# Where three small products stand in a hand-scheduled transformer layer: folded values, state products and the order of GpSimd's normalizations

## Chip, core and metric

The kernel runs on one core of a Trainium2 chip. A core has five engines that run their own instruction streams side by side: TensorE (PE in the rows; PEld is its weight load), VectorE (DVE), ScalarE (ACT), GpSimd (POOL) and SyncE (SP), which issues the DMAs. They meet only through semaphores. The metric is the device time of one execution in microseconds (us); the median of several executions counts.

## What is computed

The reference is one decoder layer over 16 batches of 512 tokens of width 256, all in float32. Three sublayers follow one another, each with a residual and a layer norm:

```python
# 1: linear attention, 16 heads of 16; K = 2 key/value sets
states = einsum('kbhnd,kbhne->kbhde', ks, vs); state = prod(states, axis=0)
out = layernorm(einsum('bhnd,bhde->bhne', q, state)) * g + b;  x = layernorm(x + out @ Wo + bo)
# 2: cross attention, 16 heads of 64, 64 context rows per batch
attn = softmax(q @ k.T * 64**-0.5);  x = layernorm(x + (attn @ v) @ Wout.T + b_out)
# 3: eight experts (256 -> 1024 -> 256) that each take the first 1024 tokens with weight > 0
x = layernorm(x + combined)
```

## The kernel before

**Stages.** A setup stage prepares weights and the context's keys and values (until about 110 us of the profile), an attention loop computes sublayers 1 and 2 (to about 880 us), and the experts follow. The change is in the attention loop.

**The loop.** It runs over batches `it`, and in each over four slots of 128 tokens, tile n = 4·it + slot. One slot of the middle of the loop does for its tile: the scores `sim` (L137 to L139, three passes of split-float products, two halves h), their maximum and difference on DVE (`dve_max` L867, `dve_shift` L872), exp on ACT (L726), sums and reciprocal `rz` on DVE (L812, L816), the multiplication by `rz` on POOL (L968, two halves, "normalizes"), and, one tile late, the transposition of the probabilities `prob` into `pt` on PE (L497, two halves, `pe_pT`), the split of `pt` into `pT_hi` (ACT) and `pT_lo` (DVE L879) and the product with the folded values into `ob` (`pe_pB`). Around it run the linear attention of a later tile (`zb`, L524 to L526), three layer norms whose statistics are DVE's (L772, L774) and whose reciprocal root is POOL's (`pool_rstd`, `pool_rstd_twice`), and transpositions of `x` (`tr`).

**Preparations.** What a whole batch shares is made piece by piece between this work: `G`, `GT`, `R`, `T1`, `T0`, `ST`, `SB`, `SW`, `Q0`, `Q1` for the linear attention two batches ahead; `A0` to `A3` the folded keys of the next batch; `B0` to `B3` the folded values (`pw<-wox,vraw`, L454), used from slot 1 of their own batch. `ST` is the state products (`pw<-wk,t_sb`, L417, 32x32 tiles of the array, small products). From them DVE makes `s` (L762), POOL `sprod` and `sbdT` (L935, L938, `pool_state`), PE `SB` and `SW` (L427, L422), ACT and DVE their split `zw_hi`, `zw_lo` (L628, L745), and `zw` is used from the next batch on. A table written out by hand, `ORDER`, gives each preparation a (slot, place) on PE, on ACT and on DVE; the slot functions `pe_slot`, `act_slot`, `dve_slot` call `prep(place)` at fixed points. A pair such as `B0`, `B1` is one group of products on PE. All preparations share two accumulation banks, `pw0` and `pw1`, by turns; each waits until DVE or ACT has emptied the one before it on its bank. So `T1` waits for `B2`'s split, and `Q0` for `SB`'s.

**Queues.** Every engine works its stream in the written order. On POOL the end of slot 2 is `pool_state`, then `xb` (L912), then slot 3 begins with `pool_rstd_twice` (L899 to L907). ACT's output norms of slot 3 (L633 to `x2` and `o_sb`) wait for its `nmr`, and the split `zw_hi` is written behind them.

Of the kernel before, what the change touches and what calls it, by code (L numbers as in the profile page):

```python
# [27 lines left out]
P = 128  # L28
# [113 lines left out]
def setup_and_attention(nc, t, k, first, kv_scr, x2_scr, mask_scr, out_rows,  # L142
                        NB, S, C, NKV, MC, TPB, PAIRS, KEYS, HEADS, CAP, ffn_sizes):
    HK = KEYS // 2
# [49 lines left out]
    s = {n: k.sem(n) for n in (  # L194
        "x_loaded", "k_loaded", "v_loaded",
        "prep_made", "prep_hi", "prep_split", "prep_copied", "state_ready", "st_prod", "r_prod", "r_summed", "wv_split", "g_split",
        "tr_made", "tr_hi", "tr_taken", "xb_ready",
        "z_made", "z_taken", "x1_ready", "x1_biased",
        "sim_made", "max_made", "sim_taken", "exp_made", "sum_made", "rz_made", "p_ready",
        "pt_made", "pt_hi_made", "pt_taken", "o_made", "o_taken",  # L200
        "x2_ready", "out_ready", "x1_ones", "mask_in_a", *(f"x2_stored{i}" for i in range(4)), *(f"out_stored{i}" for i in range(4)),
        "bst0", "bst1", "bst2", "mv0", "mv1", "mv2",
# [4 lines left out]

    ORDER = {
# [9 lines left out]
    FIRST_ORDER = {  # L218
# [85 lines left out]
    def need(eng, name, value):  # L304

        if not isinstance(value, int) or value > 0:
            eng.wait_ge(s[name], value)
# [49 lines left out]
    def tile_exists(n):  # L357
        return not isinstance(n, int) or 0 <= n < NTILES
# [170 lines left out]
    def parts(it, slot):  # L529

        n = 4 * it + slot
        isint = isinstance(it, int)
        has_sim = not isint or 0 <= it < NB
        has_z = not isint or 0 <= it + 1 < NB
        has_prev = not isint or 1 <= n <= NTILES
        has_xT = not isint or TPB <= n + 8 < NTILES
        has_x1T = not isint or 0 <= n + 3 < NTILES
        return has_sim, has_z, has_prev, has_xT, has_x1T
# [100 lines left out]
    def has_state(it):  # L639

        return within(it + 2) and not (isinstance(it, int) and it == -2)
# [219 lines left out]
    def by_head(ap):  # L861
        return ap.rearrange("p (g j) -> p g j", j=NKV)
# [20 lines left out]
    def pool_rstd(pool, ln, n, q):  # L883

        counted[f"mv{ln}"].wait_next(n + 1)
        pool.tensor_scalar(ve[:, q, ln:ln + 1], mv[:, ln, q, 1:2], EPS, None, ALU.add).then_inc(s[f"ve{ln}"], 1)  # L886
        pool.wait_ge(s[f"ve{ln}"], n + 1)

        need(pool, ("z_taken", "x1_ready")[ln], n - 1)
        pool.tensor_tensor(rstd[:, q, ln:ln + 1], ve[:, q, ln:ln + 1], epsc[:, 0:1], ALU.pow).then_inc(s[f"rstd{ln}"], 1)  # L890
        if ln:
            counted[f"rstd{ln}"].wait_next(n + 1)
            pool.tensor_scalar(nmr[:, q, ln:ln + 1], mv[:, ln, q, 0:1], rstd[:, q, ln:ln + 1], -1.0,
                               ALU.mult, ALU.mult).then_inc(s[f"nmr{ln}"], 1)

    def pool_rstd_twice(pool, n, q):

        counted["mv2"].wait_next(n + 1)
        pool.tensor_scalar(ve[:, q, 2:3], mv[:, 2, q, 1:2], EPS, None, ALU.add)  # L899
        pool.tensor_scalar(ve[:, q, 3:4], mv[:, 2, q, 1:2], 1.0 + EPS, EPS * EPS, ALU.mult, ALU.add).then_inc(s["ve2"], 1)  # L900
        pool.wait_ge(s["ve2"], n + 1)

        need(pool, "x2_ready", n - 1)
        need(pool, "out_ready", n - 1)
        pool.tensor_tensor(rstd[:, q, 2:4], ve[:, q, 2:4], epsc[:, :], ALU.pow).then_inc(s["rstd2"], 1)
        counted["rstd2"].wait_next(n + 1)
        pool.tensor_scalar(nmr[:, q, 2:4], rstd[:, q, 2:4], mv[:, 2, q, 0:1], -1.0, ALU.mult, ALU.mult).then_inc(s["nmr2"], 1)  # L907

    def pool_xb(pool, n, b, slot, q):
        need(pool, "x_loaded", 16 * (b + 1))  # L910
        need(pool, "z_taken", n - 1)
        pool.tensor_tensor(xb[:, slot % 2, :], xraw[:, q, slot, 0:C], bprime[:, :], ALU.add).then_inc(s["xb_ready"], 1)  # L912

    def pool_x1_bias(pool, n, slot, par):

        need(pool, "tr_made", n + 5)
        x1_tile = x1[:, par(1 if slot else 0), (slot - 1) % 4, 1:C + 1]
        pool.tensor_tensor(x1_tile, x1_tile, boutbc[:, :], ALU.add).then_inc(s["x1_biased"], 1)  # L918

    def pool_split(pool, it):  # L920

        need(pool, "prep_copied", number(it, "GT", COPIED))
        pool.tensor_tensor(g_lo[:, :], g_sb[:, :], f32(g_hi[:, :]), ALU.subtract)
        pool.tensor_tensor(g10_lo[:, :], g10[:, :], f32(g10_hi[:, :]), ALU.subtract).then_inc(s["g_split"], 1)

    def pool_sums(pool, it):

        need(pool, "prep_copied", number(it, "R", COPIED))
        pool.tensor_tensor(r_prod[:, :, :], wvT[:, :, :], s_bc[:, :].unsqueeze(1).broadcast_to([P, 2 * MC, C]),
                           ALU.mult).then_inc(s["r_prod"], 1)  # L930

    def pool_state(pool, it):

        need(pool, "prep_split", number(it, "ST", FINISHED))
        pool.tensor_tensor(sprod[:, :, :], s01[:, 0, :, :], s01[:, 1, :, :], ALU.mult).then_inc(s["st_prod"], 1)  # L935
        pool.wait_ge(s["st_prod"], it + 3)
        need(pool, "prep_made", number(it - 1, last_of("SW", "SB")))
        pool.tensor_tensor(sbdT[:, :, :].rearrange("p m (g e) -> p m g e", g=4),  # L938
                           sprod[:, :, :].unsqueeze(2).broadcast_to([P, MC, 4, QW]),
                           blockmask[:, :].rearrange("p (g e) -> p g e", g=4).unsqueeze(1).broadcast_to([P, MC, 4, QW]),  # L940
                           ALU.mult).then_inc(s["state_ready"], 1)

    def pool_slot(pool, it, slot, e):
        par = lambda a: (e + a) % 2
        has_sim, has_z, has_prev, has_xT, has_x1T = parts(it, slot)
        n = 4 * it + slot
        q = slot % 2
        if tile_exists(n - 2):
            pool_rstd_twice(pool, n - 2, q)
        if (it, slot) == (-1, 3):  # L950
            pool_state(pool, it)
        if it == -1:
            pool_rstd(pool, 0, n + 4, q)
        if it == -1:
            pool_rstd(pool, 1, n + 4, q)
            pool_xb(pool, n + 5, it + 1 if slot < 3 else it + 2, (slot + 1) % 4, par(1 if slot < 3 else 2))
        if (it, slot) == (-1, 3):
            for j in range(1, 4):
                pool_x1_bias(pool, n - 3 + j, j, par)
        if has_x1T and it != -1:  # L960
            pool_x1_bias(pool, n, slot, par)
        if has_z and it != -1:
            pool_rstd(pool, 0, n + 4, q)
        if has_sim:
            need(pool, "rz_made", n + 1)
            for h in range(2):
                part = by_head(prob[:, q, h * HK:(h + 1) * HK])
                pool.tensor_tensor(part, part, rz[:, q, h * 8:h * 8 + 8].unsqueeze(2).broadcast_to([P, 8, NKV]),  # L968
                                   ALU.mult).then_inc(s["p_ready"], 1)
        if has_z and it != -1:  # L970
            pool_rstd(pool, 1, n + 4, q)
        if slot == STATE_SLOT and has_state(it) and it != -1:
            pool_state(pool, it)
        if tile_exists(n + 5) and it != -1:
            pool_xb(pool, n + 5, it + 1 if slot < 3 else it + 2, (slot + 1) % 4, par(1 if slot < 3 else 2))
        if slot == SPLIT_SLOT and has_state(it):
            pool_split(pool, it)
        if slot == SUMS_SLOT and has_state(it):
            pool_sums(pool, it)
        if (it, slot) == (NB - 1, 0):  # L980
            need(pool, "prep_made", number(NB - 3, last_of("SW", "SB")))
            ff["pool_small"](pool)
        if (it, slot) == (NB - 1, 0):
            ff["pool_weights"](pool, 0, 0, 0)
# [56 lines left out]
    prob = k.sb("prob", [P, 2, KEYS])  # L1041
    mx = k.sb("mx", [P, HEADS])
    zsum = k.sb("zsum", [P, HEADS])
    rz = k.sb("rz", [P, 2, HEADS])
# [859 lines left out]
```

## Time and profile before

| | |
|---|---|
| median of 3 runs | 1239.56 us (1238.46 to 1239.6) |
| the profiled execution | 1244.09 us, span of its instructions 1242.4 us |
| busy share: PE, PEld, DVE, ACT, POOL | 97%, 85%, 69%, 45%, 47% |
| granted TensorE clock, mean | 0.99 |
| one batch in the middle, slots 0 to 3 | 12.48, 11.95, 10.93, 13.12 us |

The slot lengths are the distances between the starts of the first transposition (`pt<-ident,prob`) of each slot, here from 500.00 to 548.48 us. A busy PE is not a PE at its peak, because the ends of matmuls are modelled; the starts of consecutive instructions tell more, and a start that comes later than the usual spacing is a stall. The batches from 172 to 778 us repeat each other within 0.2 us, so one of them can be read for all.

### The profile page before, as it was taken

Reading aid. Unit: us, or ns where it says so; the run is one execution under the profiler, and the core shown is the slowest. Engines: PE = TensorE matmul, PEld = TensorE weight load, DVE = VectorE, ACT = ScalarE, POOL = GpSimd, SP = SyncE. Lnnn points to the kernel's source line nnn. Section 1 sums busy time; section 2 is a strip of 40 time slices with the busy share of each in tenths; the row PEclk is TensorE's granted clock in tenths of the full one; section 3 lists DMA queues with packets and bytes.
Section 4 is the critical chain, followed back from the end, with each engine's and each line's share of the span. In section 5 each row is a group of like instructions: output and inputs, shape, how many; then the busy total and the mean of one; then the engine's idle time right before and its main releaser. Section 6 shows DMA issues by size and latency. Waiting matters only on the chain.

```text
span 1242.4 us, 27256 instructions
## 1 busy us (share of the span) xinstructions
PE 1203.1 (97%) x10512; PEld 1051.2 (85%) x10512; DVE 863.1 (69%) x1694; ACT 555.1 (45%) x1097; POOL 585.8 (47%) x968
## 2 busy tenths in 40 slices
PE   8987999999999999999999999989999999999998
PEld 7866888888888888888888888877799899899888
DVE  5545988889889889889898898988523423432435
ACT  2124556555555555465555555545523412421420
POOL 2223665666666666656666565655322112202201
PEclk9988999999999999999999999999999999999999
DMA  9821011021111011110211111310211022021001
GB/s 274 222 65 35 12 59 54 26 60 45 35 52 53 26 61 36 43 61 19 61 44 36 52 53 35 115 50 26 95 69 69 1 69 69 1 69 69 1 1 35
DMA packets 88739, 70.07 MB, mean 56 GB/s; under 512 B 41378, under 2 KB 82083, under 8 KB 88612
## 3 DMA queue, kind: packets, MB, share of 16 engines
q1 hardware_dynamic: 86580, 67.67, 18.0%
q8 instruction: 85, 1.39, 0.5%
q10 hardware_dynamic: 2032, 0.66, 0.2%
q14 instruction: 42, 0.34, 0.1%
HBM read 42.09 MB, written 26.22 MB: 55 GB/s over the span
## 4 chain that ended last, share of the span: by engine, by line
PE 71%; DVE 8%; issue 7%; POOL 6%; ACT 1%; POOLq 0%; DVEq 0%
PE sim L137 6%; PE sim L138 6%; PE sim L139 6%; PE ob L137 5%; PE ob L138 5%; PE ob L139 5%; PE pt L497 4%; PE pw L391 3%; PE pt L139 2%; PE pt L138 2%; PE pt L137 2%; PE pw L137 2%; PE pw L454 2%; PE pw L138 2%; PE pw L139 2%
## 5 line engine op out<-in xcount | busy, mean ns | idle before, releaser
L1619 POOL TENSOR_TENSOR w_lo<-w_raw,w_hi 128x2048 fp32r<-128x2048 f32 x16 | 73.8, 4614 | 220.9 <-ACT w_hi L1559 167.8
L137 PE MATMUL ob<-b_hi,pT_hi 128*128 128x256 f32 x512 | 151.0, 295 | 0.5 <-DVE pT_lo L879 0.5
L138 PE MATMUL ob<-b_lo,pT_hi 128*128 128x256 f32 x512 | 143.6, 280 | 0.0
L139 PE MATMUL ob<-b_hi,pT_lo 128*128 128x256 f32 x512 | 143.6, 280 | 0.0
L968 POOL TENSOR_TENSOR prob<-prob,rz 128x512 f32<-128x512 f32 x128 | 131.1, 1046 | 12.6 <-DVE rz L816 12.6
L732 ACT ACTIVATE pT_hi<-pt 128x512 fp32r<-128x512 f32 x128 | 76.2, 595 | 111.2 <-PE pt L497 110.6
L726 ACT ACTIVATE prob<-prob 128x512 f32<-128x512 f32 x128 | 81.1, 633 | 99.1 <-DVE prob L872 99.0
L137 PEld LDWEIGHTS ob<-b_hi,pT_hi 128*128 128x128 f32 x512 | 96.9, 189 | 9.0 <-issue 5.4
L138 PEld LDWEIGHTS ob<-b_lo,pT_hi 128*128 128x128 f32 x512 | 97.1, 190 | 1.9
L139 PEld LDWEIGHTS ob<-b_hi,pT_lo 128*128 128x128 f32 x512 | 96.3, 188 | 0.0
L867 DVE TENSOR_REDUCE mx<-sim 128x8 f32<-128x512 f32 x128 | 87.8, 686 | 6.6 <-PE sim L139 4.4
L886 POOL TENSOR_SCALAR ve<-mv 128x1 f32<-128x1 f32 x128 | 28.0, 219 | 136.3 <-DVE mv L774 136.2
L633 ACT ACTIVATE x<-h,nmr,rstd 128x256 f32<-128x256 f32 x128 | 76.5, 598 | 34.4 <-POOL nmr L907 17.2
L497 PE MATMUL pt<-ident,prob 128*128 128x128 f32 x512 | 78.7, 276 | 13.5 <-POOL prob L968 12.0
L872 DVE TENSOR_TENSOR prob<-sim,mx 128x512 f32<-128x512 f32 x128 | 88.3, 690 | 3.9
L1594 ACT ACTIVATE hT_hi<-zb 128x512 fp32r<-128x512 f32 x30 | 17.8, 592 | 159.8 <-PE zb L139 159.8
L879 DVE TENSOR_TENSOR pT_lo<-pt,pT_hi 128x512 fp32r<-128x512 f32 x128 | 86.7, 678 | 1.9 <-ACT pT_hi L732 1.7
L497 PEld LDWEIGHTS pt<-ident,prob 128*128 128x128 f32 x512 | 59.9, 140 | 27.4 <-POOL prob L968 16.3
L918 POOL TENSOR_TENSOR x<-x,boutbc 128x256 f32<-128x256 f32 x64 | 43.9, 688 | 79.6 <-PE tr L474 75.2
L812 DVE TENSOR_REDUCE zsum<-prob 128x16 f32<-128x1024 f32 x64 | 77.8, 1215 | 4.1 <-ACT prob L726 0.7
L890 POOL TENSOR_TENSOR rstd<-ve,epsc 128x1 f32<-128x1 f32 x128 | 72.1, 563 | 10.9 <-POOL ve L886 0.2
L1838 DVE SCALAR_TENSOR_TENSOR hT_lo<-sim,hT_hi 128x512 fp32r<-128x512 f32 x62 | 42.8, 691 | 44.3 <-ACT hT_hi L1594 44.3
(244 smaller groups left out, 3726.5 us busy)
## 6 DMA issues: line engine op xcount, KB each, us to landing
xraw<-in_x SPq DMA_DIRECT2D x16, 512.0 KB, 4.0
kv_scratch<-stage SPq DMA_DIRECT2D x32, 256.0 KB, 3.6
x_scratch<-x SPq DMA_DIRECT2D x64, 128.0 KB, 1.7
out_x<-o_sb SPq DMA_DIRECT2D x64, 128.0 KB, 1.7
w_raw<-in_L_ffn_experts_inter SPq DMA_DIRECT2D x8, 1024.0 KB, 5.1
w_raw<-in_L_ffn_experts_out SPq DMA_DIRECT2D x8, 1024.0 KB, 7.8
kraw<-kv_scratch SPq DMA_DIRECT2D x16, 256.0 KB, 2.9
vraw<-kv_scratch SPq DMA_DIRECT2D x16, 256.0 KB, 2.8
```

Source lines behind the costliest of these rows:

```text
L137: pe.matmul(out, lh, rh, start=first, stop=False)
L138: pe.matmul(out, lh, rl, start=False, stop=False)
L139: return pe.matmul(out, ll, rh, start=False, stop=last)
L497: last = pe.transpose(pt[:, r * P:(r + 1) * P], prob[:, par_n, c:c + P], ident[:, :])
L633: act.activation(dst, src, ACT.Identity, bias=nmr[:, q, ln:ln + 1], scale=rstd[:, q, ln:ln + 1]).then_inc(s[done], 1)
L726: act.activation(prob[:, q, h * HK:(h + 1) * HK], prob[:, q, h * HK:(h + 1) * HK], ACT.Exp).then_inc(s["exp_made"], 1)
L732: act.activation(pT_hi[:, h * 4:h * 4 + 4, :], pt[:, :].rearrange("p (r u) -> p r u", u=P), ACT.Copy).then_inc(s["pt_hi_made"], 1)
L812: dve.tensor_reduce(zsum[:, :], prob[:, q, :].rearrange("p (g j) -> p g j", j=NKV), AX.X, ALU.add).then_inc(s["sum_made"], 1)
L867: dve.tensor_reduce(mx[:, h * 8:h * 8 + 8], by_head(sim[h][:, :]), AX.X, ALU.max).then_inc(s["max_made"], 1)
L872: dve.tensor_tensor(by_head(prob[:, q, h * HK:(h + 1) * HK]), by_head(sim[h][:, :]), mx[:, h * 8:h * 8 + 8].unsqueeze(2).broadcast_to([P, ...
L879: dve.tensor_tensor(pT_lo[:, h * 4:h * 4 + 4, :], pt[:, :].rearrange("p (r u) -> p r u", u=P), f32(pT_hi[:, h * 4:h * 4 + 4, :]), ALU.subt ...
L968: pool.tensor_tensor(part, part, rz[:, q, h * 8:h * 8 + 8].unsqueeze(2).broadcast_to([P, 8, NKV]), ALU.mult).then_inc(s["p_ready"], 1)
```

## The change

Three edits. `B0`/`B1` move on PE from between the two halves of slot 0's `ob` product to behind them, right before slot 1's first transposition, and `B2`/`B3` from between the two halves of slot 1's scores to behind them, right before its second transposition; their places on ACT and DVE move with them. `ST` moves in slot 3 in the same way, on PE and on DVE. In slot 2 POOL multiplies the first half of the probabilities by `rz` ahead of the first layer norm's root, instead of behind it.

```diff
@@ -207,12 +207,12 @@
-        "B0": ((0, 7), (0, 8), (1, 0)), "B1": ((0, 7), (0, 8), (1, 0)),
-        "B2": ((1, 1), (1, 1), (1, 3)), "B3": ((1, 1), (1, 1), (1, 3)),
+        "B0": ((0, 8), (1, 0), (1, 1)), "B1": ((0, 8), (1, 0), (1, 1)),
+        "B2": ((1, 2), (1, 3), (1, 5)), "B3": ((1, 2), (1, 3), (1, 5)),
...
-        "ST": ((3, 1), (3, 1), (3, 3)),
+        "ST": ((3, 2), (3, 1), (3, 5)),
@@ -911,6 +911,12 @@
+    def pool_p(pool, q, h):
+
+        part = by_head(prob[:, q, h * HK:(h + 1) * HK])
+        pool.tensor_tensor(part, part, rz[:, q, h * 8:h * 8 + 8].unsqueeze(2).broadcast_to([P, 8, NKV]),
+                           ALU.mult).then_inc(s["p_ready"], 1)
@@ -959,14 +965,16 @@
+        if has_sim and slot == 2:
+            need(pool, "rz_made", n + 1)
+            pool_p(pool, q, 0)
         if has_z and it != -1:
             pool_rstd(pool, 0, n + 4, q)
         if has_sim:
             need(pool, "rz_made", n + 1)
-            for h in range(2):
-                part = by_head(prob[:, q, h * HK:(h + 1) * HK])
-                pool.tensor_tensor(part, part, rz[:, q, h * 8:h * 8 + 8].unsqueeze(2).broadcast_to([P, 8, NKV]),
-                                   ALU.mult).then_inc(s["p_ready"], 1)
+            if slot != 2:
+                pool_p(pool, q, 0)
+            pool_p(pool, q, 1)
         if has_z and it != -1:
             pool_rstd(pool, 1, n + 4, q)
```

On DVE, slot 3, the piece of the difference around `s`, which DVE makes from the state products; L867 is `dve_max`, L872 `dve_shift`:

```order
 L867 TENSOR_REDUCE mx<-sim 128x8
 L872 TENSOR_TENSOR prob<-sim,mx 128x512
+L867 TENSOR_REDUCE mx<-sim 128x8
+L872 TENSOR_TENSOR prob<-sim,mx 128x512
 L762 SCALAR_TENSOR_TENSOR s<-bkq,r_sb,pw 128x32 x4
-L867 TENSOR_REDUCE mx<-sim 128x8
-L872 TENSOR_TENSOR prob<-sim,mx 128x512
 L879 TENSOR_TENSOR pT_lo<-pt,pT_hi 128x512
 L849 TENSOR_TENSOR tT_lo<-tr,tT_hi 128x512
```

The second half's maximum and difference now stand ahead of `s`. On PE in the same slot, the rows around the state products before:

```order
L138 MATMUL sim<-a_lo,tT_hi 128x512
L139 MATMUL sim<-a_hi,tT_lo 128x512
L417 MATMUL pw<-wk,t_sb 32x32 x32
L137 MATMUL sim<-a_hi,tT_hi 128x512
L138 MATMUL sim<-a_lo,tT_hi 128x512
L139 MATMUL sim<-a_hi,tT_lo 128x512
```

and of the change:

```order
L138 MATMUL sim<-a_lo,tT_hi 128x512
L139 MATMUL sim<-a_hi,tT_lo 128x512
L417 MATMUL pw<-wk,t_sb 32x32 x32
L497 MATMUL pt<-ident,prob 128x128 x4
L470 MATMUL tr<-ident,x 128x128 x2
L474 MATMUL tr<-ident,xraw 128x128 x2
```

They have the transpositions behind them now, not six more score products. On POOL, from the end of the first norm's work in slot 2 to `pool_state`, before:

```order
L918 TENSOR_TENSOR x<-x,boutbc 128x256
L886 TENSOR_SCALAR ve<-mv 128x1
L890 TENSOR_TENSOR rstd<-ve,epsc 128x1
L968 TENSOR_TENSOR prob<-prob,rz 128x512 x2
L886 TENSOR_SCALAR ve<-mv 128x1
L890 TENSOR_TENSOR rstd<-ve,epsc 128x1
L893 TENSOR_SCALAR nmr<-mv,rstd 128x1
L935 TENSOR_TENSOR sprod<-s 128x64
L938 TENSOR_TENSOR sbdT<-sprod,blockmask 128x256
```

and of the change:

```order
L924 TENSOR_TENSOR x<-x,boutbc 128x256
L917 TENSOR_TENSOR prob<-prob,rz 128x512
L886 TENSOR_SCALAR ve<-mv 128x1
L890 TENSOR_TENSOR rstd<-ve,epsc 128x1
L917 TENSOR_TENSOR prob<-prob,rz 128x512
L886 TENSOR_SCALAR ve<-mv 128x1
L890 TENSOR_TENSOR rstd<-ve,epsc 128x1
L893 TENSOR_SCALAR nmr<-mv,rstd 128x1
L941 TENSOR_TENSOR sprod<-s 128x64
L944 TENSOR_TENSOR sbdT<-sprod,blockmask 128x256
```

One of the two multiplications has moved ahead of `ve` and `rstd`; `pool_state` stays where it was.

## Rows read from the trace of the kernel before

**Rows 1.** The page: busy time, share of the span, instructions of each engine
```profile
PE 1203.1 (97%) x10512; PEld 1051.2 (85%) x10512; DVE 863.1 (69%) x1694; ACT 555.1 (45%) x1097; POOL 585.8 (47%) x968
```

**Rows 2.** Waits from 172.6 to 778.1 us: total us, times, longest
```profile
PEld pw L137 <- DVE zw_lo L745: 3.1, 12, 0.3
PE pt L497 <- POOL prob L968: 3.5, 12, 0.3
```

**Rows 3.** Timeline of PE, slot 2 into 3: start, us, instruction, [idle before]
```profile
534.79 0.28 PE L139 MATMUL ob<-b_hi,pT_lo 128*128 128x256 f32 x1
535.36 0.65 PE L497 MATMUL pt<-ident,prob 128*128 128x128 f32 x4 [0.29 <-POOL prob L968]
```

**Rows 4.** Timeline of POOL and DVE, end of slot 2
```profile
532.59 0.25 DVE L816 RECIPROCAL rz<-zsum 128x16 f32<-128x16 f32 x1
533.44 0.22 POOL L886 TENSOR_SCALAR ve<-mv 128x1 f32<-128x1 f32 x1 [2.51 <-DVE mv L774]
534.26 2.05 POOL L968 TENSOR_TENSOR prob<-prob,rz 128x512 f32<-128x512 f32 x2
535.33 0.47 DVE L856 SCALAR_TENSOR_TENSOR h<-zb,rstd,xb 128x256 f32<-128x256 f32 x1
```

**Rows 5.** Timeline of DVE, slot 3
```profile
539.39 0.71 DVE L762 SCALAR_TENSOR_TENSOR s<-bkq,r_sb,pw 128x32 f32<-128x32 f32 x4
540.02 0.68 DVE L867 TENSOR_REDUCE mx<-sim 128x8 f32<-128x512 f32 x1
...
541.35 0.68 DVE L879 TENSOR_TENSOR pT_lo<-pt,pT_hi 128x512 fp32r<-128x512 f32 x1
...
545.14 1.12 DVE L745 TENSOR_TENSOR zw_lo<-pw,zw_hi 128x256 fp32r<-128x256 f32 x2
```

**Rows 6.** Timeline of POOL and ACT, slot 3
```profile
540.19 0.32 POOL L935 TENSOR_TENSOR sprod<-s 128x64 f32<-128x64 f32 x1 [2.38 <-DVE s L762]
540.59 0.74 POOL L938 TENSOR_TENSOR sbdT<-sprod,blockmask 128x256 f32<-128x256 f32 x1
...
543.38 0.27 POOL L907 TENSOR_SCALAR nmr<-rstd,mv 128x2 f32<-128x2 f32 x1
...
543.68 0.60 ACT L633 ACTIVATE x<-h,nmr,rstd 128x256 f32<-128x256 f32 x1 [1.10 <-POOL nmr L907]
```

**Rows 7.** Timeline of PE, second part of slot 3
```profile
542.73 0.29 PE L139 MATMUL ob<-b_hi,pT_lo 128*128 128x256 f32 x1
542.85 0.39 PE L427 MATMUL pw<-ident,sbdT 128*128 128x128 f32 x2
...
545.24 0.28 PE L139 MATMUL ob<-b_hi,pT_lo 128*128 128x256 f32 x1
545.58 0.50 PE L137 MATMUL pw<-tT_hi,wq_hi 128*128 128x512 f32 x1
```

**Rows 8.** Timeline of PE: what follows tiled products, and what follows plain ones
```profile
528.82 0.66 PE L497 MATMUL pt<-ident,prob 128*128 128x128 f32 x4
529.31 0.38 PE L470 MATMUL tr<-ident,x 128*128 128x128 f32 x2
...
538.02 0.50 PE L137 MATMUL sim<-a_even_hi,tT_hi 128*128 128x512 f32 x1
538.36 0.39 PE L138 MATMUL sim<-a_even_lo,tT_hi 128*128 128x512 f32 x1
...
539.28 0.39 PE L139 MATMUL sim<-a_even_hi,tT_lo 128*128 128x512 f32 x1
539.51 0.60 PE L497 MATMUL pt<-ident,prob 128*128 128x128 f32 x4
539.95 0.38 PE L470 MATMUL tr<-ident,x 128*128 128x128 f32 x2
```

**Rows 9.** Timeline of DVE and PE, slot 1
```profile
516.14 1.29 DVE L745 TENSOR_TENSOR b_lo<-pw,b_hi 128x512 fp32r<-128x512 f32 x2 [0.23 <-ACT b_hi L628]
517.35 0.68 DVE L867 TENSOR_REDUCE mx<-sim 128x8 f32<-128x512 f32 x1
518.81 0.39 PE L137 MATMUL pw<-wv_hi,g_hi 128*128 128x512 f32 x1
```

## The prediction

> **What bounds the kernel now.** I read the page first: TensorE is busy 97% of the span and no other engine over 69% [rows 1]. So the time is that of PE's stream plus its stalls, and a change of places can only take away stalls or switching costs, or add some. Next the waits of the regular part of the loop, twelve batches. Two releasers of PE come back in every batch, 12 times each: POOL's normalized probabilities ahead of a transposition, and DVE's `zw_lo` ahead of a product of `pw` [rows 2]. Then the timeline shows where they are.
>
> The first is at the start of slot 3. After an `ob` product the next instruction normally starts 0.12 us later (542.73 to 542.85 [rows 7]); here it starts 0.57 us later (534.79 to 535.36 [rows 3]), so the stall is 0.45 us. The second is `Q0`: it starts 0.34 us behind the last `ob` product (545.24 to 545.58 [rows 7]), 0.22 more than normal. It is small, but it says that `Q0` has no slack: whatever makes `zw_lo` late makes PE late by as much.
>
> What stands ahead of `zw_lo` is a chain through four engines in slot 3. DVE makes `s` at 539.39; POOL has waited 2.38 us for it and starts `sprod` at 540.19; being in order, POOL gets to the output norm only behind `sprod`, `sbdT` and `xb`, and its `nmr` starts at 543.38; ACT has waited 1.10 us for that and starts at 543.68 the two output norms that stand ahead of `zw_hi`; DVE starts `zw_lo` at 545.14 and PE `Q0` at 545.58 [rows 5 to 7]. From `s` to `Q0` are 6.19 us, with two engines idle on the way because they waited for the link before them.
>
> **The change part by part.**
>
> *POOL first in slot 2.* `rz` is finished at 532.59 + 0.25 = 532.84, while POOL idles until the norm's statistics arrive at 533.44 [rows 4]. The first half can start at about 532.93 (0.09 us for the semaphore, an estimate, from the 0.80 us between the start of `s`, four operations of 0.71 us together, and that of `sprod` [rows 5, 6]) and is done about 1.05 us later, half of the 2.05 of the pair: 533.98 instead of 534.26 + 1.05 = 535.31. PE wants it at 534.91. The wait goes, with 0.9 us to spare: 0.45 us less in this place. Its price: `rstd` comes later. It took 0.82 us from `ve` to the next instruction (533.44 to 534.26), so it is finished at about 533.98 + 0.82 = 534.8. DVE uses it at 535.33, behind other work [rows 4]. Nothing is late. The second half starts at 534.8 and ends at 535.8, before 534.26 + 2.05 = 536.3.
>
> *The neighbours on PE.* Products on parts of the array cost something on the way in and out. A score product behind the state products takes 0.34 us to the next start (538.02 to 538.36), against 0.23 for a plain one (539.28 to 539.51): 0.11 for the way out. Where tiled products stand ahead of transpositions already (`A0` in slot 2), the four transpositions take 0.49 us (528.82 to 529.31) against 0.44 behind plain scores (539.51 to 539.95) [rows 8]: 0.05 for the way out. The way in is the same at the old places and the new. So each of the three moves is worth 0.11 - 0.05 = 0.06 us where PE doesn't wait anyway; the bounds are 0 and 0.11, and I take 0.05, since this is the nearest row, rounded down. The Trainium skill (TensorEngine Tiling (Array Packing), Key Properties) says that changing the tiling mode drains the engine, whatever the neighbour; transpositions run on the full array as the scores do, so by that rule alone the moves would be worth 0, and the sum 1.2 us worse. The trace agrees that the switch costs, and shows it cheaper ahead of transpositions.
>
> *Folded values, slots 0 and 1.* Three engines are touched, so I followed them through slot 1. `B0`/`B1` are emptied by ACT and DVE at the head of slot 1 instead of across its border; in slot 1 DVE does the same operations in another order. DVE's split of `B2`, `B3` moves behind the second maximum and difference, some 1.33 us (540.02 to 541.35 for this pair [rows 5]). `B2`'s split started at 516.14, is two of 0.6 us each (1.21 to the next start at 517.35), and `T1` on its bank starts at 518.81 [rows 9]. Moved, the first of the two runs from about 517.5 to 518.2: 0.5 us before `T1`. All else of slot 1 that PE wants is further away. I cost these moves at nothing but their two gains, 0.05 each, 0.1 us per batch, and slot 3 starts 0.1 us sooner.
>
> *State products, slot 3.* This is the part that decides. On DVE `s` now stands behind the maximum and difference of the second half. These take 1.33 us from start to the next start (540.02 to 541.35) [rows 5], and DVE has no idle time there: it runs one operation after another from the folded keys of slot 2 on, so PE's being 0.45 us sooner doesn't make DVE sooner. `s` starts at 539.39 + 1.33 - 0.09 = 540.63 (the 0.09 are the moves of slots 0 and 1). All that is behind it moves with it, since POOL and ACT waited for it before: `sprod` 541.43, `sbdT` done at 540.59 + 0.74 + 1.24 = 542.57, `nmr` 544.62, ACT's output norms 544.92, `zw_lo` 546.38, `Q0` 545.58 + 1.24 = 546.82. PE meets it twice. It arrives at `SB` at 542.85 - 0.45 - 0.09 - 0.05 = 542.26, and waits 0.3 to 0.4 us for `sbdT`; at `Q0` it arrives at about 545.2 and waits 1.6 us. The 0.45 us that POOL gained in slot 2, and the state products' own 0.05, are lost in these waits.
>
> **The sum.** A batch gets 1.33 - 0.09 = 1.24 us longer. The state is made for a batch two ahead, so slot 3 has an `ST` in the batches 0 to 13 (for the one ahead of batch 0 the table has its own places, which don't change): 14 x 1.24 = 17.4 us. In the last two batches there is no `ST`; PE waits there for the probabilities, behind DVE's work, of which the sum per slot stays the same, and I put 0 with bounds of 1 us either way. The first of the 14 may lose 0.1 less. 17.3 us on the profiled execution's 1244.09 are 1261.4; that execution lies 4.5 us above the median of the runs, so on the median it is 1239.56 + 17.3 = 1256.9.
>
> **Rivals.**
>
> *The chain has slack (faster).* If `Q0` could take `zw_lo` 1.3 us later than now, only the gains would stay: 0.45 for the stall of slot 3 and 0.15 for the three moves: 0.60 x 14 = 8.4 us, 1231.2. For it speaks that the busy shares of POOL and ACT are under half [rows 1]. Against it, that `Q0` waits 12 times of 12 for `zw_lo` [rows 2]: it decides only if the delay of `s` at DVE were under 0.45 us or so. Chance 7%.
>
> *Only part of the delay arrives.* If another operation than `s` releases ACT or POOL in part (the `xb` or the norm statistics), the delay at `Q0` could be 0.5 to 1.1 us: 7 to 15 us, 1247 to 1254. The idle times of 2.38 and 1.10 us [rows 6] speak against it, since they are as long as the whole delay. 8%.
>
> *Slot 1 gets late too.* If ACT takes `B2` later than I think, `T1` waits. The 0.5 us margin is the smallest of the replay; where it is gone and as much again is lost, each batch pays 0.5 more: 7 us, 1264. 12%.
>
> *The folded values or POOL's order do nothing at all*, or cost their bound: 0 instead of 0.09 in a batch is 1.3 us, 1258. Inside the main case.
>
> **How the numbers follow.** The forecast as worked out, 1254 to 1260, has 70%; with slot 1 late 12% (1260 to 1266), part of the delay 8% (1247 to 1254), slack 7% (1229 to 1237), and 3% for a result within 0.2%. That bound, 2.5 us, is about what a measurement of this kernel can tell from no change. The range from 1249 to 1263 leaves out the faster case, the low part of the partial one and the top of the late one. Faster 7%, same 3%, slower 90%.
>
> **What the profile of the changed kernel would show.** The wait of the transposition for POOL's probabilities at the start of slot 3 is gone, and slot 2 is 10.5 us long instead of 10.93. POOL's idle time ahead of `sprod` is about 3.6 us instead of 2.38. PE waits for POOL's `sbdT` ahead of `SB`, 0.3 to 0.4 us, and for DVE's `zw_lo` ahead of `Q0`, some 1.6 us, in 14 batches; slot 3 is 14.9 us long instead of 13.12. Slots 0 and 1 are shorter by 0.04 to 0.05 us each. The prediction is wrong if `Q0` starts less than a microsecond later within its batch, which would mean that something other than `s` sets `zw_lo`; or if `T1` waits in slot 1.

## The result and the profile after

The change made the kernel slower: 1255.65 us in the median (1254.19 to 1256.13), beside 1239.58 us (1238.46 to 1240.93) for the kernel before on the same chip. The ratio is 1.0124, 95% interval 1.0111 to 1.0136. The forecast was 1257.0, in the range 1249 to 1263. Of the executions in this document one, of `s_early`, took 1960.28 us at a mean granted clock of 0.557; its ratio leaves it out.

The page's first part, and then the waits from 173.6 to 796 us (total us, times, longest us), a stretch with twelve `Q0` and thirteen `s`. They answer to [rows 1] and [rows 2].

```profile
PE 1196.0 (95%) x10512; PEld 1046.4 (83%) x10512; DVE 861.3 (69%) x1694; ACT 547.7 (44%) x1097; POOL 585.7 (47%) x968
```

```profile
POOL sprod L941 <- DVE s L762: 48.2, 13, 3.7
...
ACT x L633 <- POOL nmr L907: 36.6, 12, 3.1
...
DVE zw_lo L745 <- ACT zw_hi L628: 21.6, 12, 1.8
...
PEld pw L137 <- DVE zw_lo L745: 18.9, 12, 1.6
PE pw L137 <- DVE zw_lo L745: 16.5, 12, 1.4
```

No engine has more work than before. PE's busy share fell from 97% to 95%, because it stands still more. `Q0` (`pw L137`) waited 3.1 us in twelve batches before, 0.26 each (PEld's row, the weight load); now 18.9 us, 1.6 each, and PE itself 1.4. The list also shows the path of the delay: POOL waits 3.7 us for `s`, ACT 3.1 for POOL's `nmr`, DVE 1.8 for ACT's `zw_hi`, PE for DVE's `zw_lo`. The wait of a transposition for POOL's `prob` [rows 2, 3] is gone from the start of slot 3.

PE in slot 3, in order of time. It answers to [rows 7] and the last part of [rows 8]:

```profile
543.40 0.76 PE L417 MATMUL pw<-wk,t_sb 128*32 128x32 f32 x64
544.09 0.66 PE L497 MATMUL pt<-ident,prob 128*128 128x128 f32 x4
544.59 0.38 PE L470 MATMUL tr<-ident,x 128*128 128x128 f32 x2
...
548.00 0.41 PE L427 MATMUL pw<-ident,sbdT 128*128 128x128 f32 x2 [0.35 <-POOL sbdT L944]
...
552.07 0.50 PE L137 MATMUL pw<-tT_hi,wq_hi 128*128 128x512 f32 x1 [1.38 <-DVE zw_lo L745]
```

The slot began at 540.11. `SB` waits 0.35 us for `sbdT`, and `Q0` 1.38 us for `zw_lo`, both where the prediction put them. The four engines between `s` and `Q0`, DVE first, then POOL and ACT:

```profile
545.92 0.71 DVE L762 SCALAR_TENSOR_TENSOR s<-bkq,r_sb,pw 128x32 f32<-128x32 f32 x4
...
551.59 1.17 DVE L745 TENSOR_TENSOR zw_lo<-pw,zw_hi 128x256 fp32r<-128x256 f32 x2 [1.80 <-ACT zw_hi L628]
```

```profile
546.71 0.33 POOL L941 TENSOR_TENSOR sprod<-s 128x64 f32<-128x64 f32 x1 [3.71 <-DVE s L762]
...
549.90 0.27 POOL L907 TENSOR_SCALAR nmr<-rstd,mv 128x2 f32<-128x2 f32 x1
...
550.20 0.60 ACT L633 ACTIVATE x<-h,nmr,rstd 128x256 f32<-128x256 f32 x1 [3.05 <-POOL nmr L907]
...
551.20 0.84 ACT L628 ACTIVATE zw_hi<-pw 128x256 fp32r<-128x256 f32 x2
```

From the start of `s` to that of `Q0` are 552.07 - 545.92 = 6.15 us; before they were 6.19. The chain is as long as it was, within 0.04 us, and it starts later: `s` 1.22 us later within its batch in the mean of 13 batches, `Q0` 1.19 us.

**Where the time is in the whole.** A batch is measured from the first transposition of its slot 0 to that of the next batch. Over the 13 distances between batches 1 and 14 the mean is 48.548 us before and 49.735 after: 13 x 1.187 = 15.4 us. From the start of slot 1 of batch 0 to the start of batch 1 come 1.3 us more (37.25 instead of 35.97), the end of the program gives 0.8 back: 15.9, where the medians differ by 16.1. The 0.8 are in the two last batches, 0.1 in batch 14 and 0.7 in batch 15: there slot 1 takes 9.64 us instead of 10.61 and slot 2 11.04 instead of 10.72. `folded_only` and `st_back` show the same pair (9.65 and 11.05 us), so it comes from the folded values' places. Before, PE waited in that slot for the split of the probabilities; of the change no such wait is in the trace:

```profile
852.10 0.39 PE L137 MATMUL ob<-b_hi,pT_hi 128*128 128x256 f32 x1 [0.54 <-DVE pT_lo L879]
```

This sum leaves out the time up to the first slot 1, which differs between executions by several microseconds whatever the kernel (last section). For this reason the table goes by batches as well as by medians. The interval is that of the ratio to the kernel before, which ran again beside each group: median 1239.80 us beside `st_back`, `s_early`, `st_only` and `norm_first`, 1240.93 beside `s_half`, `pool_only`, `norm_first_before` and `norm_first_s_early`, 1238.96 beside the others.

| kernel | batch, us | slots 0 to 3, us | median, us | ratio, 95% |
|---|---|---|---|---|
| before | 48.548 | 12.49 11.98 10.96 13.12 | 1239.58 | |
| the change | 49.735 | 12.37 12.01 10.50 14.86 | 1255.65 | 1.0124 (1.0111 to 1.0136) |
| st_back | 48.455 | 12.38 12.01 10.50 13.57 | 1239.01 | 0.9986 (0.9970 to 1.0003) |
| s_early | 48.455 | 12.38 12.01 10.50 13.57 | 1237.46 | 0.9982 (0.9964 to 0.9999) |
| st_only | 49.881 | 12.52 11.98 10.96 14.43 | 1258.71 | 1.0148 (1.0119 to 1.0177) |
| s_half | 49.463 | 12.49 11.98 10.96 14.04 | 1253.85 | 1.0104 (1.0084 to 1.0123) |
| pool_only | 48.549 | 12.48 11.98 10.51 13.58 | 1239.64 | 0.9997 (0.9985 to 1.0009) |
| folded_only | 48.458 | 12.38 12.01 10.94 13.13 | 1236.76 | 0.9977 (0.9967 to 0.9986) |
| norm_first_before | 48.548 | 12.49 11.98 10.96 13.13 | 1239.81 | 1.0003 (0.9988 to 1.0017) |
| norm_first_s_early | 48.458 | 12.38 12.01 10.50 13.58 | 1235.43 | 0.9968 (0.9953 to 0.9983) |
| norm_first | 48.092 | 12.37 12.01 10.50 13.21 | 1233.79 | 0.9951 (0.9933 to 0.9969) |
| norm_first_again | 48.104 | 12.38 12.01 10.50 13.22 | 1232.63 | 0.9946 (0.9932 to 0.9961) |
| tr_first | 47.785 | 12.38 12.01 10.50 12.90 | 1227.83 | 0.9912 (0.9892 to 0.9932) |

### The profile page after: what moved, and what is told of

The parts are those of the page before. It is cut to its first block, busy times and chain, and to the rows that moved or that the text cites. A ratio compares the mean times of both kernels' runs of the same rounds, so it can differ in the third digit from the quotient of the medians.

```text
span 1254.0 us, 27256 instructions
## 1 busy us (share of the span) xinstructions
PE 1196.0 (95%) x10512; PEld 1046.4 (83%) x10512; DVE 861.3 (69%) x1694; ACT 547.7 (44%) x1097; POOL 585.7 (47%) x968
## 4 chain that ended last, share of the span: by engine, by line
PE 67%; POOL 10%; issue 9%; DVE 6%; ACT 3%; POOLq 0%; DVEq 0%
PE sim L137 6%; PE sim L138 6%; PE sim L139 6%; PE ob L137 5%; PE ob L138 5%; PE ob L139 5%; PE pw L391 3%; PE pt L497 3%; PE pw L137 3%; PE pt L139 2%; PE pt L138 2%; PE pt L137 2%; PE pw L454 2%; PE pw L139 2%; PE pw L138 2%
## 5 line engine op out<-in xcount | busy, mean ns | idle before, releaser
L137 PE MATMUL ob<-b_hi,pT_hi 128*128 128x256 f32 x512 | 149.5, 292 | 0.0
L137 PEld LDWEIGHTS ob<-b_hi,pT_hi 128*128 128x128 f32 x512 | 96.9, 189 | 2.9
L867 DVE TENSOR_REDUCE mx<-sim 128x8 f32<-128x512 f32 x128 | 87.5, 684 | 6.4 <-PE sim L139 4.4
L872 DVE TENSOR_TENSOR prob<-sim,mx 128x512 f32<-128x512 f32 x128 | 88.3, 690 | 3.9
L139 PE MATMUL pt<-w_hi,hT_lo 128*128 128x256 f32 x256 | 72.1, 281 | 0.0
```

The source lines that it names most:

```text
L137: pe.matmul(out, lh, rh, start=first, stop=False)
L139: return pe.matmul(out, ll, rh, start=False, stop=last)
L867: dve.tensor_reduce(mx[:, h * 8:h * 8 + 8], by_head(sim[h][:, :]), AX.X, ALU.max).then_inc(s["max_made"], 1)
L872: dve.tensor_tensor(by_head(prob[:, q, h * HK:(h + 1) * HK]), by_head(sim[h][:, :]), mx[:, h * 8:h * 8 + 8].unsqueeze(2).broadcast_to([P, ...
```

## The experiments

The theory is that of the prediction: `s` is late on DVE, POOL's queue passes this on to the output norm, and all of it arrives at `Q0`. The rivals are that the state products cost by their place on PE, that only a part of the delay arrives, and that slot 1 or POOL's new order is the cause.

### The state products back in both places, and on DVE alone

`st_back` is the change with `ST` as before; `s_early` leaves `ST` at its new place on PE and takes only DVE's `s` back.

```diff
-        "ST": ((3, 2), (3, 1), (3, 5)),
+        "ST": ((3, 1), (3, 1), (3, 3)),    st_back
+        "ST": ((3, 2), (3, 1), (3, 3)),    s_early
```

> The change, with the state products and s back in their old places on PE and DVE. If the chain from s to Q0 is the whole cause, slot 3's wait for sbdT and the long wait for zw_lo go; Q0 then starts where the unchanged chain lets it, about 0.09 us sooner per batch than before (the folded values' gain), and POOL's 0.45 us is still not seen, because Q0 already waited for zw_lo before. 14 x 0.07 to 0.09 = about 1 us: 1238 to 1239 (slots 0 to 3 about 12.37, 12.0, 10.48, 13.55). Rival, the folded values or POOL's order cost something: then 1242 or more. Rival, the chain had slack and POOL's gain is real once the state products are back: 0.45 + 0.1 in 14 batches, 1231 to 1233.

> The change, with only DVE's place of s put back ahead of the second maximum; PE keeps the state products behind the scores. It tells the order on DVE from the order on PE. If DVE's order is the cause: PE finishes the products about 0.4 us before DVE wants them, so s starts as in the kernel before, and the time is that of st_back within 1 us, 1238 to 1240. If the place on PE is the cause (products late or an expensive switch of the array), it stays at 1254 to 1256.

Both give a batch of 48.455 us, 1.280 less than the change and equal to each other within 0.001. So the place on PE is worth nothing to the batch, and the whole loss hangs on the two operations that were put ahead of `s`. `s_early`'s median, 1237.46 us, lies 0.5 below what I had expected (1238 to 1240). `st_back` from `s` to `Q0` (its slot 3 starts at 532.17):

```profile
536.65 0.71 DVE L762 SCALAR_TENSOR_TENSOR s<-bkq,r_sb,pw 128x32 f32<-128x32 f32 x4
...
539.61 0.38 PE L427 MATMUL pw<-ident,sbdT 128*128 128x128 f32 x2
...
542.84 0.50 PE L137 MATMUL pw<-tT_hi,wq_hi 128*128 128x512 f32 x1 [0.57 <-DVE zw_lo L745]
```

The same of `s_early` on PE (its slot 3 starts at 532.12):

```profile
539.50 0.38 PE L427 MATMUL pw<-ident,sbdT 128*128 128x128 f32 x2
...
542.80 0.50 PE L137 MATMUL pw<-tT_hi,wq_hi 128*128 128x512 f32 x1 [0.64 <-DVE zw_lo L745]
```

In `st_back` `s` and `Q0` start 6.19 us apart, as before. But `Q0` waits 0.57 us, more than before: slot 2 is 0.46 us shorter and slot 3 0.45 longer. What POOL saves in slot 2, PE stands still in slot 3. The same happens to the little that the new place of the state products does save: in `s_early` PE is at `SB` 7.38 us behind the slot's start instead of 7.44, and waits 0.64 us at `Q0` instead of 0.57.

### The state products alone

The kernel before with only `ST` at its new places.

```diff
-        "ST": ((3, 1), (3, 1), (3, 3)),
+        "ST": ((3, 2), (3, 1), (3, 5)),
```

> The kernel before, with only the state products and s at their new places. If the chain is the cause: s 1.33 us later in 14 batches, all of it at Q0, 14 x 1.33 = 18.6, minus nothing: 1257 to 1259, slower than the whole change by 1 to 3 us, and the stall of 0.45 us for the probabilities at the start of slot 3 is still there. If the three edits share the loss, it is clearly under 1255.

A batch is 1.333 us longer in the mean. One of the 13 distances has 0.43 us more in slot 0 than the others (50.33 us; cause unknown); without it the batch is 1.30 us longer. That is the start-to-start time of the moved pair (1.33 [rows 5]) less the 0.03 us by which the chain from `s` to `Q0` is shorter in the mean (6.17 us instead of 6.19). The median is 1.0148 times that before: this third of the change is worse alone than the whole. The slot's two old waits show what happens to the stall ahead of it:

```profile
539.65 0.65 PE L497 MATMUL pt<-ident,prob 128*128 128x128 f32 x4 [0.30 <-POOL prob L968]
...
551.15 0.50 PE L137 MATMUL pw<-tT_hi,wq_hi 128*128 128x512 f32 x1 [1.40 <-DVE zw_lo L745]
```

POOL's 0.30 is still there, and `Q0` waits as long as in the full change.

### Half of the delay

The kernel before, with `s` behind the second maximum but ahead of the second difference. A price with a threshold would show less than the delay here.

```diff
-        "ST": ((3, 1), (3, 1), (3, 3)),
+        "ST": ((3, 1), (3, 1), (3, 4)),
...
             dve_max(..., 1)
+        prep(4)
             dve_shift(..., 1)
```

> The kernel before, with s on DVE behind the second maximum but ahead of the second difference: half of the way, 0.72 us instead of 1.33. PE is untouched. If Q0's start follows s one to one, without slack: 14 x 0.72 = 10 us, 1249 to 1251, batch 49.27 us. If there is a threshold (some slack, then loss), it lies clearly below 10 us, or at nothing.

```profile
544.03 0.69 DVE L868 TENSOR_REDUCE mx<-sim 128x8 f32<-128x512 f32 x1 [0.26 <-PE sim L139]
544.63 0.71 DVE L762 SCALAR_TENSOR_TENSOR s<-bkq,r_sb,pw 128x32 f32<-128x32 f32 x4
...
550.79 0.50 PE L137 MATMUL pw<-tT_hi,wq_hi 128*128 128x512 f32 x1 [0.94 <-DVE zw_lo L745]
```

My expectation of `s` missed: it is 0.95 us later within its slot (4.98 instead of 4.03 us behind the slot's start), not 0.72, because the maximum, no longer behind `s`, is early and waits 0.26 us for PE's scores. The batch is 0.915 us longer, and the median, 1253.85, lies above my 1249 to 1251 for that reason. So the rule holds at a second size: 0.95 us of delay gave 0.915, and 1.33 gave 1.30. There is no threshold between.

### POOL's order alone, and the folded values alone

The kernel before with the edit of `pool_slot` alone, and with the places of `B0` to `B3` alone.

```diff
+        if has_sim and slot == 2:
+            need(pool, "rz_made", n + 1)
+            pool_p(pool, q, 0)                                             pool_only
...
-        "B0": ((0, 7), (0, 8), (1, 0)), ...  "B2": ((1, 1), (1, 1), (1, 3)), ...
+        "B0": ((0, 8), (1, 0), (1, 1)), ...  "B2": ((1, 2), (1, 3), (1, 5)), ...   folded_only
```

> The kernel before, with POOL's new order in slot 2 alone. The wait of 0.45 us at the start of slot 3 goes, slot 2 is 10.5 us. If Q0 is held by zw_lo and that by DVE's chain from slot 2, slot 3 gets as much longer: batch 48.55, 1239 to 1240, no change. If PE's own stream is the bound there, the gain is 0.45 x 14 = 6 us: 1233.

> The kernel before, with the folded values' new places alone. By the traces so far they are worth 0.09 us per batch, because the products stand next to transpositions: slot 0 at 12.37 to 12.38 instead of 12.49, slot 1 at 12.0 instead of 11.97, batch 48.46 instead of 48.55; 1.3 us in all, less than the runs can tell, 1237 to 1240. If what st_back gained came from POOL's order, the batch stays at 48.55.

`pool_only` shortens slot 2 by 0.45 us and lengthens slot 3 by 0.46; the batch is unchanged (48.549), the ratio 0.9997. The reason stands at `Q0`, whose weight load waited 0.26 us before and waits 0.78 now (6.2 us in eight batches, 300 to 700 us); PE itself waits 0.57:

```profile
541.09 0.50 PE L137 MATMUL pw<-tT_hi,wq_hi 128*128 128x512 f32 x1 [0.57 <-DVE zw_lo L745]
```

`folded_only` gains 0.090 us in a batch, all in slot 0 (-0.11), while slot 1 loses 0.03. The ratio is 0.9977, and its interval leaves out 1. The Trainium skill (TensorEngine Tiling (Array Packing), Key Properties) says that a change of tiling mode drains TensorE, and names no neighbour on which the price depends; by that alone this run would show 0. It shows a small gain instead, of the size of two moves at 0.05. The medians differ by 2.2 us, of which 14 batches explain 1.3; another 0.6 is in the last batch's slots 1 and 2, as told above.

### The output norm ahead of `s` in POOL's queue

If POOL's queue is what passes the delay on, it must vanish when the norm of slot 3 stands ahead of `sprod`. `norm_first` is the change with `pool_state` moved from the end of slot 2 to behind `pool_rstd_twice` in slot 3; `norm_first_before` makes the same edit in the kernel before.

```diff
-        if (it, slot) == (-1, 3):
+        if (it, slot) == (-1, 3) or slot == 3 and has_state(it):
             pool_state(pool, it)
...
-        if slot == STATE_SLOT and has_state(it) and it != -1:
-            pool_state(pool, it)
```

> The change, with POOL's pool_state moved behind the output norm of slot 3, so that the norm doesn't wait for s. If the chain from s to Q0 runs through POOL's order (s, sprod, sbdT, xb, norm, ACT's output norms, zw_hi, zw_lo), nmr2 comes before s, ACT is free when SB and SW are made, and Q0 starts when PE gets there: its wait of 1.4 to 1.6 us goes. PE still waits 0.35 us for sbdT. A batch is then 49.74 - 1.6 = 48.1 us, faster than before: 14 x (48.55 - 48.1) = 6 us less than before, 1232 to 1235. If zw_lo is late for another reason (the state products themselves, or DVE's own load), most of the wait stays and it is over 1245.

> The kernel before, with pool_state behind slot 3's output norm and nothing else. There zw_lo starts at 545.14 right behind DVE's own statistics, though zw_hi is there at the same time; DVE stood idle 0.59 us before it split tT, waiting for ACT. If that idle time is a second limit on zw_lo, as near as POOL's: no change, 1238.5 to 1240. If POOL's order is the only limit before the change too: 0.22 us per batch, 3 us, 1236.5.

`norm_first` is 1.643 us per batch faster than the change, and with 0.9951 faster than the kernel before. POOL, DVE and PE in its slot 3, which starts at 526.95:

```profile
531.90 0.27 POOL L907 TENSOR_SCALAR nmr<-rstd,mv 128x2 f32<-128x2 f32 x1
532.76 0.71 DVE L762 SCALAR_TENSOR_TENSOR s<-bkq,r_sb,pw 128x32 f32<-128x32 f32 x4
534.02 0.69 DVE L849 TENSOR_TENSOR tT_lo<-tr,tT_hi 128x512 fp32r<-128x512 f32 x1
534.84 0.41 PE L427 MATMUL pw<-ident,sbdT 128*128 128x128 f32 x2 [0.34 <-POOL sbdT L944]
...
537.37 0.40 PE L137 MATMUL pw<-tT_hi,wq_hi 128*128 128x512 f32 x1
```

`nmr` starts 0.86 us ahead of `s`, not 3.98 behind it. `Q0` no longer waits; what is left of the late `s` is PE's 0.34 us at `SB`.

`norm_first_before` changes nothing at all (48.548): of the two outcomes that I had named, no change and 3 us less, it is the first. There a second limit is as near as the one taken away:

```profile
535.29 0.69 DVE L849 TENSOR_TENSOR tT_lo<-tr,tT_hi 128x512 fp32r<-128x512 f32 x1 [0.59 <-ACT tT_hi L722]
```

DVE idles 0.59 us ahead of `tT_lo`, because ACT's `tT_hi` stands behind the exp of the second half, whose difference DVE makes only behind `s`. In the change DVE makes that difference first, and the gap is filled. Two further kernels take this up.

### Which of the two limits holds: `s` early again, and ACT's order

`norm_first_s_early` is `norm_first` with DVE's `s` back at (3, 3). `tr_first` is that kernel with ACT's transposition copy `tT_hi` ahead of its second exp, so that a late difference doesn't matter to `tT_lo`. `norm_first_again` repeats `norm_first` beside it.

```diff
+        if slot == 3:
+            act_tr(act, n, slot, has_x1T, has_xT)
             act_exp(act, n, q, 1)
...
-        if slot == 3:
-            act_tr(act, n, slot, has_x1T, has_xT)
```

> norm_first with s back at its early place on DVE. PE's wait for sbdT (0.35 us) goes. But the trace of st_back shows DVE idle 0.58 us ahead of the split of tT when s stands early, because ACT's exp and tT_hi wait for the second difference, which s delays; with s late that gap is filled. If this is the next limit, zw_lo starts 10.2 us after slot 3's start instead of 9.6, Q0 waits again, slot 3 is 13.5 instead of 13.2: 1237 to 1239, worse than norm_first by 4. If only the wait for sbdT counts, it is better than norm_first: 1228 to 1230.

> norm_first_s_early, with ACT's tT_hi of slot 3 ahead of its second exp. If DVE's idle 0.58 us ahead of the split of tT is what holds zw_lo there, it goes, zw_lo starts 9.65 us after slot 3's start instead of 10.22, and Q0 at 10.1, with no wait for sbdT ahead: slot 3 about 13.0, batch 47.87, 14 x 0.68 = 9.5 us less than before, 1229 to 1231, and better than norm_first by 3. If exp then comes late and sums with it, the gain is lost: 1235.

> norm_first once more, beside tr_first on the same chip: 1232 to 1235, batch 48.09.

`norm_first_s_early` falls back to 48.458: the gap on DVE is there again, and `Q0` waits 0.63 us. Its median, 1235.43, is lower than the 1237 to 1239 that I had expected; the batch is as expected (slot 3 13.58 us). DVE and PE:

```profile
536.06 0.69 DVE L849 TENSOR_TENSOR tT_lo<-tr,tT_hi 128x512 fp32r<-128x512 f32 x1 [0.59 <-ACT tT_hi L722]
...
538.58 0.99 DVE L745 TENSOR_TENSOR zw_lo<-pw,zw_hi 128x256 fp32r<-128x256 f32 x2
...
539.03 0.50 PE L137 MATMUL pw<-tT_hi,wq_hi 128*128 128x512 f32 x1 [0.63 <-DVE zw_lo L745]
```

`tr_first` takes the gap away with `s` early; its ACT, and then DVE and PE:

```profile
528.47 0.59 ACT L722 ACTIVATE tT_hi<-tr 128x512 fp32r<-128x512 f32 x1
529.41 0.63 ACT L726 ACTIVATE prob<-prob 128x512 f32<-128x512 f32 x1 [0.35 <-DVE prob L872]
```

```profile
529.29 0.68 DVE L879 TENSOR_TENSOR pT_lo<-pt,pT_hi 128x512 fp32r<-128x512 f32 x1
529.89 0.68 DVE L849 TENSOR_TENSOR tT_lo<-tr,tT_hi 128x512 fp32r<-128x512 f32 x1
...
532.85 0.50 PE L137 MATMUL pw<-tT_hi,wq_hi 128*128 128x512 f32 x1
```

`tT_lo` follows the row ahead of it without a gap. `Q0` starts 10.00 us behind the start of slot 3 (522.85), where `norm_first_s_early` has 539.03 - 528.36 = 10.67. The batch is 47.785 us: 0.673 less than `norm_first_s_early`, from which it differs in ACT's order alone, 0.32 less than `norm_first_again`, measured beside it, and 0.763 less than before. With 0.9912 and a median of 1227.83 (I had expected 1229 to 1231) it is the fastest kernel of the study. POOL's order in slot 2 and the folded values came with the change. ACT's order alone, without the norm moved ahead, was not run.

## Why the prediction was right, by its steps

The prediction named as its own refutation a `Q0` that starts less than a microsecond later within its batch, or a wait at `T1`. `Q0` starts 1.19 us later in the mean, and `T1` does not wait.

**`s` behind the pair, 1.33 us.** Shown. `s_early` takes back DVE's place alone and with it all of the loss; `st_only` costs 1.30 (1.333 with its one longer batch).

**The chain hands it on one to one through POOL's queue.** Shown: at two sizes by `st_only` and `s_half`, and for the place by `norm_first`, where the same late `s` no longer reaches `Q0`. The rival that only a part arrives falls.

**The folded values and neighbours, 0.05 for each move.** Right in the sum, wrong in the places. The prediction says 0.04 to 0.05 for each of slots 0 and 1; slot 0 gave 0.11 to 0.12 and slot 1 lost 0.03. In slot 0 the `ob` product behind `B0`, `B1` took 0.22 us to the next start, where plain ones take 0.12, and that is saved. But the first transposition of slot 1 and that behind `B2` come after tiled products now, and take longer to the next start than before. Before:

```profile
510.96 0.38 PE L137 MATMUL ob<-b_hi,pT_hi 128*128 128x256 f32 x1
511.18 0.28 PE L138 MATMUL ob<-b_lo,pT_hi 128*128 128x256 f32 x1
...
512.48 0.60 PE L497 MATMUL pt<-ident,prob 128*128 128x128 f32 x4
512.83 0.48 PE L137 MATMUL sim<-a_even_hi,tT_hi 128*128 128x512 f32 x1
...
516.90 0.60 PE L497 MATMUL pt<-ident,prob 128*128 128x128 f32 x4
517.33 0.38 PE L470 MATMUL tr<-ident,x 128*128 128x128 f32 x2
```

The change:

```profile
517.63 0.66 PE L497 MATMUL pt<-ident,prob 128*128 128x128 f32 x4
518.04 0.48 PE L137 MATMUL sim<-a_even_hi,tT_hi 128*128 128x512 f32 x1
...
522.02 0.66 PE L497 MATMUL pt<-ident,prob 128*128 128x128 f32 x4
522.52 0.38 PE L470 MATMUL tr<-ident,x 128*128 128x128 f32 x2
```

The first is 0.41 us from the next start instead of 0.35, the second 0.50 instead of 0.43. So the price at the exit of `B0`, `B1` moved from slot 0 into slot 1 and fell from 0.10 to 0.06 us; that of `B2`, `B3` fell from 0.11 to 0.07 within slot 1.

**Slot 1 late at `T1`.** It did not happen. `B2`'s split is the first of the two `b_lo` that start at 522.81, and `T1` on its bank starts at 524.01, without a wait:

```profile
522.81 1.28 DVE L745 TENSOR_TENSOR b_lo<-pw,b_hi 128x512 fp32r<-128x512 f32 x2
524.01 0.39 PE L137 MATMUL pw<-wv_hi,g_hi 128*128 128x512 f32 x1
```

**POOL first in slot 2.** The stall went and the slot is 10.50 us, as said, and the gain is lost at `Q0`. But the prediction lost it to the late `s`, and its rival "slack" gave it back: 0.60 us a batch if the delay did not count. That was wrong. With `ST` at its old places the 0.45 us are lost as well (`pool_only`, `st_back`), since `Q0` waited already [rows 2, 7]; the kernel could have gained 0.09, not 0.60. The rows for it were in hand: a stall ahead of a wait on a chain that does not run through it only lengthens that wait.

**The sum.** 1.24 us per batch was forecast and 1.19 measured, so 14 batches gave 16.7, not 17.4. The 0.05 are at both ends of the chain: `s` starts 1.22 us later within its batch, and from there to `Q0` it is 0.04 us less than before. The change against `st_only` is 0.146 us shorter in a batch; 0.09 come from the folded values and 0.03 from `st_only`'s one longer batch, and 0.02 are open. The state products' own exit, which the prediction called lost, is lost as it says: `s_early` has it at `SB` (7.38 us instead of 7.44) and no longer at `Q0`. For the last two batches the prediction put 0 with bounds of 1 us; they gave 0.8 back, through a wait in batch 15 which it did not look at. One bound of a rival is off by its own numbers: 14 x 1.1 on 1239.56 is 1255, not 1254. Nothing hangs on it.

## What to carry to other kernels

Before an operation is moved, look at what stands behind its consumer in that engine's queue: here `sprod` was not urgent, but a layer norm with nothing to do with it stood behind it in POOL's order, and so 1.33 us on DVE became 1.30 us of TensorE in each of the 14 batches. A stall taken away is a gain only if the next wait on that engine has slack; if the next wait is on a chain through other engines, the stall moves there whole. If a fix does nothing, look for a second limit at the same distance: in `norm_first_before` and `norm_first_s_early` it was a copy behind an exp, and the norm's new place paid only when that limit went too, with `s` behind the difference (`norm_first`) or with the copy ahead of the exp (`tr_first`).

## What the runs showed of the hardware

**The start differs from one execution to the next.** Slot 1 of batch 0 starts at 124.16 us in the profiled execution of before, at 119.86 in that of the change, and between 116.80 and 122.15 in the others, though the kernels hardly differ ahead of it; `norm_first` and `norm_first_again`, the same kernel, have 119.78 and 116.80. The batches of that pair differ by 0.012 us. The granted clock falls there from 2.4 to 1.2 GHz, in stretches that differ between the executions. Before, and then `folded_only`, in a window of 10 us (length, busy PE, PEld, DVE, ACT, POOL, granted clock, DMA share, GB/s); the two are not at the same instruction there:

```profile
85.00:95.00 10.00, 7.33 (x24) 5.83 (x23) 3.70 (x9) 1.52 (x4) 7.71 (x13) 0.66 0.00 0
```

```profile
85.00:95.00 10.00, 6.27 (x91) 5.09 (x90) 4.94 (x13) 1.73 (x4) 7.93 (x14) 1.00 0.00 0
```

**The last two batches differ too.** Slot 2 of batch 14 in `norm_first` and then in `norm_first_again`, the same kernel:

```profile
801.90:813.90 12.00, 11.95 (x181) 10.28 (x182) 9.55 (x19) 6.26 (x12) 6.29 (x14) 0.86 0.15 24
```

```profile
799.10:809.50 10.40, 10.35 (x181) 9.29 (x182) 9.49 (x19) 6.26 (x12) 6.26 (x13) 1.00 0.17 27
```

The same products take 11.90 us at a mean granted clock of 0.86 and 10.33 at 1.00. The start's 3.0 us and these 1.6 are the difference between the two profiled executions (1230.9 and 1226.6 us of span), within 0.3. The profiled executions of before and of the change both have the low clock in slot 0 of batch 15 (9.96 and 9.88 us at 0.83) and not in batch 14, so the comparison of their ends above is a fair one; in `folded_only` that slot takes 8.34 us at 1.00. Why the clock falls in one execution and not in another is open: ahead of that slot PE had stood still for the probabilities in both, 2.59 us before and 2.55 us in `folded_only`. Medians of equal batches can differ by as much: `norm_first_s_early` and `st_back` have 48.458 and 48.455 us and medians 3.6 us apart. For effects of a microsecond the batch length is the better measure.

**A stall of 1.4 us in each batch did not cost clock.** The change's granted clock is 1.00 from 111 us to the end of batch 14, though PE stands still ahead of every `Q0`:

```profile
111.00:846.00 735.00, 704.42 (x7207) 609.43 (x7205) 636.39 (x1271) 394.07 (x832) 453.64 (x837) 1.00 0.15 46
```
